# Second norm's rows: from VectorE to ScalarE, with scale and bias made by GpSimd

## The reference, cut to what matters

```python
def _layernorm(x, axis=-1, eps=1e-05):
    m = jnp.mean(x, axis=axis, keepdims=True)
    v = jnp.var(x, axis=axis, keepdims=True)
    return (x - m) / jnp.sqrt(v + eps)

mod = (_silu(L0_c) @ L0_wmod).reshape(L0_c.shape[0], 6, 1, -1)
h = _layernorm(x) * (1 + ca) + sa
x = x + ga * _L0_attn_ref(h, ...)          # 16 heads of 64, causal softmax, gates
h = _layernorm(x) * (1 + cb) + sb          # the second norm
x = x + gb * _L0_ffn_ref(h, ...)           # gated MLP + product-key experts (top 8 of 512)
```

## Time and profile before

| | |
|---|---|
| three runs | 1470.13, 1471.36, 1471.42 us; median 1471.36 |
| the profiled execution, own time | 1472.29 us |
| its span | 1470.4 us, 1.9 us less than its time |
| granted TensorE clock, mean | 0.999 of full |
| busy: PE, DVE, ACT, POOL | 96%, 92%, 85%, 70% of the span |
| the chain that ended last: PE, DVE, issue, ACT | 63%, 25%, 6%, 5% |
| DMA | 19 GB/s over the span |
| length of a turn of the loop | 44.14 us (the L1100 pair starts at 693.49 and at 737.63) |

### The profile page before, as it was taken

The page is one execution under the profiler, slowest core; times in us unless marked ns, Lnnn a source line. Parts: engine busy times, 40 slices in busy tenths (PEclk is TensorE's granted clock), DMA queues, the critical chain, the costliest instruction groups (busy, mean ns, idle before and its releaser), DMA issues.

```text
span 1470.4 us, 39693 instructions
## 1 busy us (share of the span) xinstructions
PE 1410.8 (96%) x11491; PEld 1158.4 (79%) x11491; DVE 1355.9 (92%) x5409; ACT 1253.1 (85%) x4130; POOL 1036.0 (70%) x1157
## 2 busy tenths in 40 slices
PE   6899999999999999999999999999999999999988
PEld 4678778878778888778888778888778888778878
DVE  5689999999999999999999999999999999999988
ACT  5798888898888898888898888898888898888883
POOL 2057778777778777778777778777778777778760
PEclk9999999999999999999999999999999999999999
DMA  4000000000000000000000000000000000000000
GB/s 130 15 16 20 16 9 20 20 17 19 14 9 20 20 17 19 14 9 20 20 16 19 14 9 20 20 16 19 14 9 20 20 16 20 14 9 23 10 14 10
DMA packets 50753, 27.74 MB, mean 19 GB/s; under 512 B 10304, under 2 KB 49920, under 8 KB 50720
## 3 DMA queue, kind: packets, MB, share of 16 engines
q1 hardware_dynamic: 50480, 26.91, 7.0%
q10 hardware_dynamic: 240, 0.43, 0.1%
HBM read 23.02 MB, written 4.31 MB: 19 GB/s over the span
## 4 chain that ended last, share of the span: by engine, by line
PE 63%; DVE 25%; issue 6%; ACT 5%; DVEq 0%; DMA 0%; POOL 0%; SPq 0%; POOLq 0%
PE pS L1444 9%; PE pW L1376 9%; PE pW L1378 7%; PE pW L1377 7%; PE pW L1457 6%; PE pS L1434 5%; DVE h L1100 5%; DVE pS L1017 4%; PE pS L1430 4%; ACT pS L639 4%; PE pW L1525 4%; PE pW L1528 4%; PE pW L1461 2%; PE pW L1516 2%; DVE p_sb L1037 2%
## 5 line engine op out<-in xcount | busy, mean ns | idle before, releaser
L639 ACT ACTIVATE pS<-pS,nmx 128x128 f32<-128x128 f32 (+1 forms) x1024 | 391.1, 440 | 53.4 <-DVE nmx L1017 53.4
L499 POOL TENSOR_TENSOR fexp<-fexp,fsum 128x512 f32<-128x512 f32 x240 | 300.4, 1285 | 76.6 <-DVE fexp L1138 76.6
L1017 DVE CUSTOM_DVE_ANT_0 pS<-pS,mask 128x128 f32<-128x128 f32 (+1 forms) x1024 | 330.1, 389 | 18.8 <-PE pS L1434 18.0
L490 POOL TENSOR_TENSOR fsum<-ex 128x512 f32<-128x512 f32 x248 | 250.8, 1050 | 0.0
L631 ACT COPY pT<-pS 128x768 f32<-128x768 f32 x256 | 211.6, 827 | 34.6 <-PE pS L1444 30.7
L1444 PE MATMUL pS<-ident,p_sb 128*128 128x128 f32 x1536 | 214.9, 276 | 5.3 <-DVE p_sb L1037 3.3
L1037 DVE TENSOR_TENSOR p_sb<-pS,coef 128x256 f32<-128x256 f32 (+2 forms) x512 | 210.4, 452 | 8.9
L1444 PEld LDWEIGHTS pS<-ident,p_sb 128*128 128x128 f32 x1536 | 172.1, 140 | 36.1 <-issue 17.0
L639 ACT ACTIVATION_READ_ACCUMULATOR pS<-pS,nmx 128x1 f32 x1024 | 199.9, 195 | 0.0
L621 ACT COPY qk<-pW 128x512 f32<-128x512 f32 x256 | 166.5, 650 | 2.2 <-PE pW L1378 2.2
L1457 PE MATMUL pW<-pT,v 128*64 128x256 f32 x1024 | 165.4, 401 | 0.3 <-ACT pT L631 0.2
(11 more groups left out here) (201 smaller groups left out, 3716.2 us busy)
## 6 DMA issues: line engine op xcount, KB each, us to landing
x_in<-in_L_attn_tokens SPq DMA_DIRECT2D x32, 128.0 KB, 2.1
x_res<-in_L_attn_tokens SPq DMA_DIRECT2D x32, 128.0 KB, 3.0
modB<-mods_dram SPq DMA_DIRECT2D x32, 128.0 KB, 2.9
modA<-mods_dram SPq DMA_DIRECT2D x31, 128.0 KB, 3.1
out<-yo SPq DMA_DIRECT2D x31, 128.0 KB, 1.9
modC<-mods_dram SPq DMA_DIRECT2D x32, 64.0 KB, 3.1
fsum<-in_L_attn_Wkv SPq DMA_DIRECT2D x2, 512.0 KB, 7.4
fsum<-in_L_attn_Wq SPq DMA_DIRECT2D x1, 512.0 KB, 5.5
```

Of the source, the lines that this page charges most:

```text
L490: ins = nc.gpsimd.tensor_tensor(fsum[:, k, h], ex[:, k, h, 0:NX].unsqueeze(2).broadcast_to([P, NX, NK]), ex[:, k, RH + h, :].unsqueeze(1). ...
L499: ins = nc.gpsimd.tensor_tensor(fexp[:, k, h, :], fexp[:, k, h, :], fsum[:, k, h].rearrange("p i j -> p (i j)"), ALU.mult)
L639: ins = nc.scalar.activation(ps, ps, ACT.Exp, bias=nmx[:, p % 2, h, k:k + 1], scale=-1.0, accum_out=den(p)[:, h, k:k + 1])
L1017: ins = nc.vector.tensor_tensor_reduce(out=ps, in0=ps, in1=mask[:, (1 - k) * P:2 * P], scale=-1.0, scalar=LARGEST, op0=ALU.add, op1=ALU.mi ...
```

## The change

The two row instructions of `ln2_modulate` leave DVE. ACT makes the same rows as Identity(scale * x2 + bias) with scale = rs2 and bias = -mean * rs2, two instructions of 128x128 from SBUF to SBUF with both scale and bias read from a column. POOL makes that bias in two more instructions of 128x2: the negated means right behind the epsilon, and their product with rs2 at the end, behind one more wait of POOL on its own result. In ACT's list the step stands behind `scale_head(3)` and ahead of `gate_up(3)`; in the drain behind `gate_up(3)` and ahead of `diagonals(1)`. `transpose_h` on PE waits on the same semaphore as before, now raised by ACT.

```diff
-        pool_chain1, pool_chain2 = ev("pool_chain1", 2), ev("pool_chain2", 1)
+        pool_chain1, pool_chain2 = ev("pool_chain1", 2), ev("pool_chain2", 2)
...
                 def rstd2():
-                        nc.gpsimd.tensor_scalar(ve2[:, :], mv2[:, :, 1], LN_EPS, None, ALU.add).then_inc(S(pool_chain2), 1)
+                        nc.gpsimd.tensor_scalar(ve2[:, :], mv2[:, :, 1], LN_EPS, None, ALU.add)
+                        nc.gpsimd.tensor_scalar(nm2[:, :], mv2[:, :, 0], -1.0, None, ALU.mult).then_inc(S(pool_chain2), 1)
                         pool.wait_ge(S(pool_chain2), at(pool_chain2, f, 1))
-                        nc.gpsimd.tensor_tensor(rs2[:, :], ve2[:, :], expo[:, :], ALU.pow).then_inc(S(rstd2_out), 1)
+                        nc.gpsimd.tensor_tensor(rs2[:, :], ve2[:, :], expo[:, :], ALU.pow).then_inc(S(pool_chain2), 1)
+                        pool.wait_ge(S(pool_chain2), at(pool_chain2, f, 2))
+                        nc.gpsimd.tensor_tensor(mr2[:, :], nm2[:, :], rs2[:, :], ALU.mult).then_inc(S(rstd2_out), 1)
...
+                def rows2():
+                    if w.live(-1):
+                        act.wait_ge(S(rstd2_out), at(rstd2_out, f, 1))
+                        for k in range(TB):
+                            ins = nc.scalar.activation(h2[:, k, :], x2[:, k, :], ACT.Identity, bias=mr2[:, k:k + 1], scale=rs2[:, k:k + 1])
+                        ins.then_inc(S(h2_ready), 1)
...
                     gate_up(3)
+                    rows2()
                     diagonals(1)
...
                 scale_head(3)
+                rows2()
                 gate_up(3)
...
-                def ln2_modulate():
-                    if w.live(-1):
-                        dve.wait_ge(S(rstd2_out), at(rstd2_out, f, 1))
-                        for k in range(TB):
-                            ins = nc.vector.tensor_scalar(h2[:, k, :], x2[:, k, :], mv2[:, k, 0:1], rs2[:, k:k + 1], ALU.subtract, ALU.mult)
-                        ins.then_inc(S(h2_ready), 1)
...
                     pick(0, 2)
-                    ln2_modulate()
                     gated_down(1)
...
                 ln1_stats()
-                ln2_modulate()
                 bias_product(3)
```

More of the change, by code:

```diff
@@ L131, in program @@
         rs2 = sb("rs2", [P, TB])
+        nm2 = sb("nm2", [P, TB])
+        mr2 = sb("mr2", [P, TB])
         h2 = sb("h2", [P, TB, D])
```

## The result

The changed kernel takes 1452.97 us (median of 4 runs) against 1471.39 before: a ratio of 0.9872, interval 0.9857 to 0.9887. It is faster by 1.3%; 1453.9 was forecast.

What follows compares the result with a forecast made beforehand. PE was taken to lead, busy 1410.8 us of 1470.4, its idle time being what can be won. Per turn 0.24 + 0.39 = 0.63, times 30 = 18.9, less 1.4 = 17.5 us, giving 1453.9; range 1445 to 1466.

Steps and rivals of the forecast that it cites:

- the forecast's own case: Whole kernel: 0.45 to 0.90 us gained a turn, 1446 to 1459 us; chance 0.60.
- lost in the drain: Last stretch, once: GpSimd's bias comes later and ACT's diagonals(1) stand behind the rows, so modulate_h is late; loss 1.4 us.
- What the change removes: DVE loses 2.32 us a turn; the low part of h2T comes earlier and similarity(0) on PE stops waiting; gain 0.39.
- turn 1: The turn where POOL has no such products yet and PE does not wait for h2; used as a ready-made experiment.
- What is late next: PE's scores(5) waits for ACT's copy of the transposes; of 0.47 us won at the transposes of h2, 0.24 is left.
- rival 2: All of PE's idle time goes, small waits too: at most 0.98 us a turn, 1443.4 us; chance 0.10.
- POOL's two instructions: POOL's two 128x2 additions take 0.56 us, hidden by its wait for the mean squares; bias ready 0.67 before ACT asks.
- Rival 1: ACT's pair costs 1.08 us, so the copy is later: 0.25 a turn, 1465 us; sign: PE waits over 0.4; chance 0.15.
- Rival 4: Slower: POOL's additions take over 1.23 us, so ACT waits for the bias and scores(5) is late; middle some 1480; chance 0.09.
- The last sign: Would show the forecast wrong: another DVE instruction stretched to over a microsecond beside POOL's products.

Runs made afterwards that it cites:

- e2: The kernel before, with the two row instructions of the second norm left out (h2 filled with ones once): 1442.80 us, ratio 0.9799.
- e5: The kernel before, with one wait added: GpSimd's weigh(1), four 128x512 products, starts only when VectorE has made the rows of h2: 1475.13 us, ratio 1.0023.
- e1: The kernel before, with GpSimd's two added instructions alone; nobody reads their result and VectorE makes the rows as before: 1457.43 us, ratio 0.9907.
- e10: The kernel before, with the rows of h2 made ahead of the first norm's statistics on VectorE and nothing else: 1459.1 us, ratio 0.9912.
- e11: The kernel before, with the wait of e5 and the rows of h2 on VectorE ahead of normalise(3): 1445.03 us, ratio 0.9816.

## Why the prediction was right, and where it was not

**The number** was right (1453.9; 1453.0), within the forecast's own case: 0.69 us a turn for 0.63, and 1.2 lost in the drain for 1.4.

**What the change removes.** Right: DVE loses the pair, waits 1.44 us for gate_up(3) instead, and is busy 39.7 us a turn (39.6 forecast); the wait of similarity(0) goes, 3.40 to 3.00, for 0.39 forecast from turn 1. A further 0.08 of that wait was not counted: PE's first step inside similarity(0) falls from 0.31 to 0.23, in e2 as in the changed kernel. That POOL's products stretch the rows was argued from turn 1; e5 shows it (336 ns with POOL held back).

**What is late next.** Right in kind, 0.29 us off in size. scores(5) was to follow scores(4) by 1.46 us (1.70 less 0.24) and follows by 1.75, so this term was a loss of 0.05 and no gain. In the turn shown it is 1.79, and the 0.33 there can be read off the rows: ACT reaches the new step 0.07 later against scores(4), the pair takes 0.77 and not 0.70, queries(5) and the copy take 1.40 and not 1.28, and scores(5) starts 0.14 behind the copy and not 0.08. On the pair the Trainium skill ("ScalarE: Activation LUTs", What ACT_TABLE_LOAD costs) was nearer: the estimate from its page was 0.77, and the trace agrees.

**What was costed at nothing and was not.** The forecast had no gain outside these two places and named it only as rival 2. ET(1) comes 0.18 earlier, and between similarity(0) and similarity(1) a second 0.08 is won at project_v(5), whose first step falls from 0.27 to 0.18: 0.26 a turn together. In e2, where PE does not wait at scores(5), the two give only 0.02. So it is no separate gain but the other side of the missed term: while PE stands for the copy, the others catch up. For ET(1) the way can be followed: in the turns shown POOL takes up DVE's mean squares 2.47 us behind the start of similarity(1), for 2.64 before, and fold(1) comes behind them. The sum closes: 0.40 + 0.08 + 0.26 - 0.05 = 0.69. The errors, 0.29 too much in one term and 0.34 left out in others, cancelled; this part of the agreement was luck.

**POOL's two instructions** were taken to be hidden, with 0.56 us of delay. The bias is ready 0.74 later than the deviation was, and the products start 0.71 later (both counted from the epsilon), since the negation puts the power 0.45 later and not 0.24, and the product with its wait adds 0.29 for 0.32; the bias comes 0.54 ahead of ACT's need for a forecast 0.67. In the changed kernel they are hidden. But that a delay of POOL can also gain time was left out: with the rows still on DVE these two instructions alone gain 0.53 us a turn (e1), where the whole change gains 0.69, because they shift the products against the rows. The prediction took the rows' 2.32 us for a price that only their removal saves. It was the price of one place in POOL's steps, and e10 and e11 get 0.5 and 0.9 us a turn back without moving anything to another engine.

**The rivals.** Rival 1 (the copy late by more) had its sign appear: PE waits for the copy by more than 0.4 us (0.50 in the row shown). Its cause did not, for the pair costs 0.77 and not 1.08, and the term is -0.05 a turn, between the forecast's 0.24 and the rival's -0.14. So that sign could not tell the two apart. Rival 2 had the 0.98 us as its ceiling; e2 finds 0.96. Rival 4 needed the bias to come over 0.67 later than forecast against ACT's need; it came 0.13 later, still 0.54 ahead. The last sign, another DVE instruction over a microsecond beside POOL's products, stands in both kernels: the thresholding of the experts, 0.54 us otherwise, is over a microsecond in 30 of its 240 executions before and after (longest 1.50 and 1.49). The rows were not the only work that POOL stretched, and this part was neither counted nor tried.

```profile
L1145 DVE TENSOR_SCALAR fexp<-fsum,top,rz x240: 534/542/1492, 101.8 to 1377.8; 128x512 f32<-128x512 f32 x120
```

## What to carry to other kernels

When the same instruction takes three times as long in one place as in another, first ask which engine works beside it, and try to move the two apart before moving the work: an order of steps and one wait gave 1.8% here, the change 1.3%. A delay of the other engine can be a gain, so cost it on both sides of nothing, and look where its later work lands: the same collision waits at the next such instruction (e5). Of a wait that is put on the leading engine, part is given back where it had waited for others, so terms read off one place do not simply add up round a loop.

## What the runs showed of the hardware

- The row instruction on VectorE, 128x128 from SBUF to SBUF with two column scalars (340 ns alone), that meets GpSimd's 128x512 products gets in only as one of them ends, and takes up to 1.32 us. The thresholding of 128x512, also from SBUF to SBUF, goes from 0.54 to 1.49 us at worst. The pair took 2.32, 1.79 and 0.60 us when it started 1.51, 0.81 us into them, or ahead of them. The Trainium skill ("GPSIMD Engine Reference", 8. Key points) says that GpSimd and VectorE contend for SBUF where VectorE's instruction is in a two-port mode or has two SBUF inputs; the trace agrees that they contend, and adds how long; in which mode the row instruction ran, no run shows.
- Not all of VectorE is hit: the statistics of the first norm (L928 in e1, also from SBUF) run beside a product in the same 0.48 us for two in e1, before, and in the changed kernel. In e1:

```profile
729.50 0.48 DVE L928 BATCH_NORM_STATS2 st<-x_in 128x6 f32<-128x128 f32 x2
```

- In the kernels before and after, GpSimd's 128x2 arithmetic took 0.19 to 0.39 us, its power 0.69 to 0.86. The one exception is the epsilon in the drain, 0.57 in both.
